# Megakernel of state space mixer and experts: one region of SBUF shared by all stages takes the first operands of the following stage, and the last stage's weights are split as a 33rd expert

## What is computed

```
x1  = x + tanh(g_x) * mamba(ctx, gate = layernorm(x))       # selective scan, 1024 channels x 16 states
xn  = layernorm(x1)
ffn = 2 * sum over 4 chosen of 32 experts (w1, w3: 1024x512; w2: 512x1024; at most 256 rows in each)
      + shared expert (w_sg, w_su: 1024x1024; w_sd: 1024x1024)
out = x1 + tanh(g_f) * ffn
```

## Time and profile before

| what | value |
|---|---|
| median of three runs | 4308.99 us |
| profiled execution, its own time | 4307.87 us |
| its span in the profile | 4306.1 us |
| TensorE busy | 3887.4 us (90%) |
| VectorE busy | 3074.7 us (71%) |
| ScalarE busy | 2147.3 us (50%) |
| GpSimd busy | 1800.7 us (42%) |
| barrier passed into the scan | 567.15 us |
| into the first shared pass | 1842.42 us |
| into the experts (first issue of SP) | 2539.66 us |
| into the second shared pass | 3725.18 us |

### The profile page before, as it was taken

How to read it: one execution, slowest core, us unless ns; L and a number is a source line. 1 busy time by engine, 2 the same in 40 slices (tenths; PEclk the granted TensorE clock), 3 DMA queues, 4 the chain that set the end, 5 groups by cost and what they waited for, 6 DMA issues and landing times. The chain is left out here.

```text
span 4306.1 us, 59367 instructions
## 1 busy us (share of the span) xinstructions
PE 3887.4 (90%) x21088; PEld 3143.6 (73%) x21088; DVE 3074.7 (71%) x3700; ACT 2147.3 (50%) x2213; POOL 1800.7 (42%) x1010
## 2 busy tenths in 40 slices
PE   8877548888988889869999979999999999899999
...
GB/s 230 215 232 225 181 219 118 106 200 118 108 209 107 138 181 114 89 189 187 188 171 182 192 179 243 234 229 230 232 230 231 229 232 232 174 293 249 200 161 122
DMA packets 327334, 817.74 MB, mean 190 GB/s; under 512 B 66112, under 2 KB 108352, under 8 KB 317952
## 3 DMA queue, kind: packets, MB, share of 16 engines
...
...
## 5 line engine op out<-in xcount | busy, mean ns | idle before, releaser
L926 POOL TENSOR_TENSOR h<-h,c 128x1024 f32<-128x1024 f32 x512 | 1206.4, 2412 | 54.8 <-DVE h L909 52.1
L909 DVE TENSOR_TENSOR_SCAN h<-da,dbu 128x1024 f32<-128x1024 f32 x512 | 1134.7, 2273 | 74.1 <-ACT dbu L875 51.4
L943 PE MATMUL psb<-m,du_taps 128*128 128x128 f32 x4096 | 581.5, 290 | 130.2 <-ACT dbu L875 80.4
L943 PEld LDWEIGHTS psb<-m,du_taps 128*128 128x128 f32 x4096 | 511.0, 196 | 197.5 <-ACT dbu L875 109.2
L882 ACT ACTIVATE da<-dl,ad 128x1024 f32<-128x1024 f32 x512 | 589.6, 1151 | 79.5 <-DVE h L909 67.4
L953 PE MATMUL psy<-ident,h 128*128 128x128 f32 x4096 | 562.1, 281 | 46.5 <-POOL h L926 27.0
L875 ACT ACTIVATE dbu<-psb 128x1024 f32<-128x1024 f32 x512 | 523.1, 1022 | 83.6 <-PE psb L943 72.1
L1822 DVE TENSOR_TENSOR wsp<-raw,wsp 128x2048 fp32r<-128x2048 f32 x192 | 434.1, 2289 | 106.7 <-ACT wsp L1775 106.7
L953 PEld LDWEIGHTS psy<-ident,h 128*128 128x128 f32 x4096 | 447.6, 143 | 81.4 <-POOL h L926 54.2
L1662 POOL DMA_INDIRECT xg<-scratch_xn,ids x64 | 63.6, 993 | 1054.8 <-PE psT L1682 1033.0
L1775 ACT ACTIVATE wsp<-raw 128x2048 fp32r<-128x2048 f32 x192 | 359.1, 1910 | 17.4 <-DMA raw<-in_w 16.9
...
## 6 DMA issues: line engine op xcount, KB each, us to landing
raw<-in_w SPq DMA_DIRECT2D x192, 1024.0 KB, 6.9
du_taps<-scratch_duT SPq DMA_DIRECT2D x512, 128.0 KB, 2.9
scratch_duT<-duT SPq DMA_DIRECT2D x64, 512.0 KB, 2.7
c<-scratch_c SPq DMA_DIRECT2D x64, 512.0 KB, 8.7
...
scratch_ob<-ob SPq DMA_DIRECT2D x64, 512.0 KB
...
xz<-in_x SPq DMA_DIRECT2D x32, 512.0 KB, 5.6
```

The source lines that it names most:

```text
L909: dve.tensor_tensor_scan(h[:, k % HR, :], da[k % 2][:, :], dbu[:, (k // GN) % 2, k % GN, :], 0.0, ALU.mult, ALU.add).then_inc(s_scan, 1)
L926: pool.tensor_tensor(h[:, k % HR, :], h[:, k % HR, :], c[:, n, :], ALU.mult).then_inc(s_hc, 1)
L943: mm = pe.matmul(psb[:, j], duT[:, r * CP + j, :], m[:, g // 2, :, r * CP + j, g % 2 * GN:(g % 2 + 1) * GN], start=True, stop=True)
```

## The change

- A region `arena` of 48 KB in each partition is allocated once and kept. In stage 1 it holds `w_in` and `ctxT`; in stage 2 the first half of the matrix (`m0`, 32 KB) and the taps (16 KB) lie in its place; in stage 3 `raw` and the token tiles `xt` and `xin`; in stage 4 `raw` and the transposed rows; in stage 5 `y` and the transposed tokens. `ident` is loaded once, in stage 1.
- Stage 1, in drain steps, all from SP: at step 33 `zero_matrix` (zeros to `m0`, 4 MB, from the 1 KB of `zero`), at steps 36 and 37 `first_du` (1 MB each, two DMAs), at step 40 `first_matrix` (8 DMAs of 128 KB). In the scan the second half `m1` is zeroed by GpSimd and loaded behind c[0] to c[2].
- Stage 2, last unit, before its last store: `first_weights` (4 MB) and `first_tokens` (four tiles, 2 MB).
- Stage 3, before the stores of tile 30: `first_expert`, w1 and w3 of expert 0 (4 MB).
- Stage 4: the second half of the shared expert is loaded and split as expert 32, its third matrix at an additional place in the last expert; the first transposed tokens are loaded after the last up product. `wsp` is handed on to stage 5, which splits nothing, and its memset of `y` waits for nothing.
- The semaphores of the early loads are cleared once, at the end.

In the diff's middle parts `early`, once the name of a flag in `split`, becomes `second`; those lines and some of names and waits are cut.

```
+            def zero_matrix():
+
+                sp.wait_ge(s_psx, Q)
+                sp.wait_ge(s_zero, 1)
+                sp.dma_start(f32(m0[:]).rearrange("p (r z) -> p r z", z=ROW), zero[:].unsqueeze(1).to_broadcast([P, TB, ROW])).then_inc(s_mz, 16)
+
+            def first_matrix():
+
+                sp.wait_ge(s_mz, 16)
+                sp.wait_ge(s_btst, 4 * P // TB * 16)
+                for dst_, src_ in matrix_blocks(f32(m0[:]).rearrange("p (t r) -> p t r", t=TB), dr, 0, 0):
+                    sp.dma_start(dst_, src_).then_inc(early["m"], 16)
+
+            def first_du(part):
+
+                for q in s_dust:
+                    sp.wait_ge(q, 16)
+                for twin in range(2):
+                    sp.dma_start(f32(taps[part * 2 * TB + twin:(part + 1) * 2 * TB:2]), dr["duT"][0, twin]).then_inc(early["du"], 16)
+
             def step(s):
                 on_tile(s, LOG + 1, store_delta)
+                if s == Q + 1:
+                    zero_matrix()
+                if s == Q + 4:
+                    first_du(0)
+                if s == Q + 5:
+                    first_du(1)
+                if s == Q + 8:
+                    first_matrix()
...
+def matrix_blocks(m, dr, b, half):
+
+    for part in range(2):
+        for a in range(TB // BAND):
+            band = dr["bT"][b, part, half]
+            rows = bass.AP(band.tensor, band.offset + a * BAND * SKEW, [[BAND * ROW, 2 * BAND], [1, BAND * ROW]])
+            p0 = part * 2 * TB + a * 2 * BAND
+            yield m[p0:p0 + 2 * BAND, a * BAND:(a + 1) * BAND].rearrange("p t r -> p (t r)"), rows
...
-        m = sb("m", [P, 2, TB, NC, NH], F32R)
-        duT = sb("du_taps", [P, NC, P], F32R)
+        m0, m1 = m0[:], sb("m", [P, TB * ROW], F32R)[:]
+        m = [v.rearrange("p (t c n) -> p t c n", t=TB, c=NC) for v in (m0, m1)]
...
+            def first_weights():
+
+                sp.wait_ge(s_mm, (NU - 1) * NST + NH)
+                for mat, src_ in enumerate((io["w_sg"], io["w_su"])):
+                    for half in range(2):
+                        w0 = (2 * mat + half) * KH * HB // 2
+                        sp.dma_start(arena[:, w0:w0 + KH * HB // 2].rearrange("p (k f) -> p k f", k=KH // 2),
+                                     src_[:, 0:HB].rearrange("(h k p) f -> h p k f", h=2, p=P)[half]).then_inc(early["w3"][mat][half], 16)
+
+            def first_tokens():
+
+                sp.wait_ge(s_mm, SETS)
+                sp.wait_ge(s_gst, 16 * ET)
+                for t in range(2):
+                    for i, src_ in enumerate((dr["gated"], io["x"])):
+                        w0 = 2 * KH * HB + (2 * i + t) * H
+                        sp.dma_start(arena[:, w0:w0 + H], src_.rearrange("b (t p) h -> (b t) p h", p=P)[t]).then_inc(early["x"][t], 16)
+
             load_delta(0)
-            for r in range(PARTS):
-                load_du(0, r)
-            load_m(0, 0)
-            load_c(0, 0)
+            for n in range(3):
+                load_c(0, n)
             load_m(0, 1)
-            for n in range(1, NST):
+            for n in range(3, NST):
                 load_c(0, n)
...
+                if final:
+                    first_weights()
+                    first_tokens()
...
             act.dma_start(gate[:], io["g_x"].partition_broadcast(P)).then_inc(s_c, 16)
-            act.dma_start(ident[:], io["ident"]).then_inc(s_c, 16)
-            act.wait_ge(s_c, 32)
+            act.wait_ge(s_c, 16)
             act.activation(gate[:], gate[:], ACT.Tanh).then_inc(s_gate, 1)
...
-            dve.memset(f32(m[:, 0]), 0.0).then_inc(s_zero, 1)
...
-            pool.memset(f32(m[:, 1]), 0.0).then_inc(s_zero, 1)
+            pool.memset(f32(m1), 0.0).then_inc(s_zero, 1)
...
-            pe.wait_ge(s_c, 32)
...
                 if g == 0:
-                    pe.wait_ge(s_du[r], i * 64 + 64)
-                if k % (ET * NST) in (0, NH):
-                    pe.wait_ge(s_m[k % (ET * NST) // NH], (i // ET + 1) * 2 * TB // BAND * 16)
+                    if i:
+                        pe.wait_ge(s_du[r], i * 64)
+                    elif r == 0:
+                        pe.wait_ge(early["du"], 64)
+                half = k % (ET * NST) // NH
+                if k == 0:
+                    pe.wait_ge(early["m"], 2 * TB // BAND * 16)
+                elif k % (ET * NST) in (0, NH):
+                    pe.wait_ge(s_m[half], (i // ET + half) * 2 * TB // BAND * 16)
...
-            consts = [(gate[:], io["g_f"].partition_broadcast(P)), (ident[:], io["ident"])]
+            consts = [(gate[:], io["g_f"].partition_broadcast(P))]
...
-            load(0, 0)
+            cols = slice(0, HB)
             if route:
-                load(1, 1)
-            cols = slice(part * HB, (part + 1) * HB)
-            for m, src in enumerate((io["w_sg"][:, cols], io["w_su"][:, cols], io["w_sd"][cols, :])):
...
                 for half in range(2):
-                    if m == 2:
-
-                        sp.wait_ge(s_wlo, half + 1)
-                    sp.dma_start(raw[:, m % 2, halves[half]].rearrange("p (k f) -> p k f", k=blocks),
-                                 src.rearrange("(h k p) f -> h p k f", h=2, p=P)[half]).then_inc(s_raw[m % 2][half], 16)
+
+                    sp.wait_ge(s_wlo, half + 1)
+                    sp.dma_start(raw[:, 0, halves[half]].rearrange("p (k f) -> p k f", k=KF // 2),
+                                 io["w_sd"][cols, :].rearrange("(h k p) f -> h p k f", h=2, p=P)[half]).then_inc(s_raw[half], 16)
             if route:
                 sp.wait_ge(s_init, 1)
                 sp.dma_start(dr["tab"].rearrange("(p s) o -> p (s o)", p=P), zero[:]).then_inc(s_tab, 16)
...
+            def first_expert():
+
+                sp.wait_ge(s_wlo, 6)
+                for m, src in enumerate((io["w1"], io["w3"])):
+                    for half in range(2):
+                        sp.dma_start(raw[:, m, halves[half]].rearrange("p (k f) -> p k f", k=KH // 2),
+                                     src[0].rearrange("(h k p) f -> h p k f", h=2, p=P)[half]).then_inc(early["w4"][m][half], 16)
+
...
+                    if route and known and t == TT - 2:
+                        first_expert()
...
-                    pool.wait_ge(s_x[par], j * 32 + 32)
+                    if isinstance(j, int) and j == 0:
+                        pool.wait_ge(early["x"][par], 32)
+                    else:
+                        pool.wait_ge(s_x[par], j * 32)
...
-                pool.wait_ge(s_wlo, 6)
...
-                    if first:
+                        if known and t == 0:
+                            pe.wait_ge(early["xT"], 16)
+                        else:
+                            pe.wait_ge(s_x[par], j * 16 + 16 * par)
+                    if route and first:
...
             if route:
                 x_head(0, 0, 0)
-            for m in range(3):
-                for half in range(2):
...
+            if route:
+                for m in range(3):
...
-                src = (io["w1"], io["w3"], io["w2"])[m][e].rearrange("(h k p) f -> h p k f", h=2, p=P)
+                if isinstance(e, int) and e == NE:
+                    src = (io["w_sg"][:, HB:FS], io["w_su"][:, HB:FS], io["w_sd"][HB:FS, :])[m]
+                else:
+                    src = (io["w1"], io["w3"], io["w2"])[m][e]
+                src = src.rearrange("(h k p) f -> h p k f", h=2, p=P)
...
-            load_matrix(0, 0, 0)
-            sp.dma_start(ident[:], io["ident"]).then_inc(s_c, 16)
...
-            load_matrix(0, 0, 1)
             load_matrix(0, 0, 2)
             load_matrix(1, 1, 0)
...
-                    load_matrix(e + 1, x + 1, 1)
-                    load_matrix(e + 1, x + 1, 2)
-                if not (known and e + 2 >= NE):
+                load_matrix(e + 1, x + 1, 1)
+                load_matrix(e + 1, x + 1, 2)
+                if not (known and e + 2 > NE):
                     load_matrix(e + 2, x + 2, 0)
+                if known and e == NE - 1:
+
+                    sp.wait_ge(s_u, TPE * NE)
+                    sp.dma_start(xT[:, 0].bitcast(F32), dr["xT"][0]).then_inc(early["xT"], 16)
                 store_rows(e, 0)
...
-                    act.wait_ge(s_raw[c][half], ((3 * e + m) // 2) * 16 + 16)
+                    if isinstance(e, int) and e == 0 and m < 2:
+                        act.wait_ge(early["w4"][m][half], 16)
+                    else:
+                        act.wait_ge(s_raw[c][half], ((3 * e + m) // 2) * 16)
...
-                if not last:
-                    matrix_head(e + 1, x + 1, 0)
+                matrix_head(e + 1, x + 1, 0)
                 silu(e, 1)
-                if not last:
-                    matrix_head(e + 1, x + 1, 1)
+                matrix_head(e + 1, x + 1, 1)
...
+                if last:
+                    matrix_head(e + 1, x + 1, 2)
...
-                if not last:
-                    for half in range(2):
-                        matrix_rest(e + 1, x + 1, 0, half)
```

(36 more changed lines are left out.)

99 lines of the change are left out of this document (45 added, 54 removed).

## The result

Over four runs each, the kernel after took 4251.88 us (4248.17 to 4255.61) and the kernel before 4308.65 us (4304.97 to 4309.22): the ratio is 0.987, with a 95% interval of 0.9853 to 0.9887. In the profiled executions the span falls from 4306.1 to 4253.8 us, by 52.3.

What follows compares the result with a forecast made beforehand. TensorE, busy 90% of the span, paces shared passes and experts, VectorE and GpSimd the scan; only stage boundaries could gain. Terms -19.3 +1.0 +0.5 +2.8 -2.4 -5.0 -13.6 +2.7 +0.5 gave -32.8: 4276 us, range 4269 to 4291.

Steps and rivals of the forecast that it cites:

- Scan, the gain: Barrier into the scan to first scan: first matrix and taps already in place, first scan at +15.0 for +34.3, -19.3 us.
- Scan, the price: End of stage 1: new SP transfers delay the stores behind them; zeros +1.0, taps +0.5, matrix +2.8 us.
- rival (a): End of stage 1: zeros crawl at 131 GB/s, price 21 us in place of 1, time 4296; chance 0.08.
- First shared pass: Head of stage 3: loads removed, norm earlier, but last gated store lands later behind the preloads; -2.4 us (-6 to +1).
- experts: Head of stage 4: first transpose waits for the gather, no longer for the identity; -5.0 us (-3 to -6).
- second pass: Head of stage 5: first product needs only gate and transposed tokens, 3727.5 in place of 3741.12; -13.6 us.
- the last expert: End of stage 4: third split of the 33rd expert delays the copy of psO; +2.7 us (0 to 5).
- (c): Rival: preloads given back where issued, every upper price at the other steps, 9 us dearer, time 4285; chance 0.22.
- (b): Rival, end of stage 1: zeros so slow that the kernel gets slower, at 60 GB/s about 4335 us; chance 0.03.
- (d): Rival, scan's head: c rows or u hold the ladder, 2 to 6 us more, 4281; 0.65 together with the forecast.
- (e): Rival, stage boundaries: no change, because stages hide their heads; chance 0.02.
- the third sign: Sign of being wrong: TensorE stays longer at the lower clock in the new heads than in the old; same loss assumed.

## Why the prediction was wrong

**The step that failed** is the sentence in the first part that "inside the stages nothing of the change could help much", because TensorE sets the pace there. That it sets the pace was right, and is the reason why the change helped: with TensorE busy 350.00 of 350.00 us, anything that makes one product cheaper goes straight to the end. I took the duration of a product as a property of its shape, 128x128 with 512 columns, and counted what was added, removed and moved in time, but not what was moved in space. The change lays every tile of stages 3 to 5 anew. One pair, `xT_place` and wsp, came to stand at the same place within 256 bytes, and its 4,608 products went from 233 to 227 ns: 26 of the 52.3 us. Moving one against the other by 32 bytes undoes it, moving both keeps it, and giving the other pairs the same distance gains some 16 us more. No row of the kernel before could price it, as all its pairs stood 32 bytes off; that the layout was changed under the engine that bounds three stages could have been named as a case, and wasn't.

**Scan, the gain** (-19.3, measured -18.6): right. The 0.7 is the gate's load: I took 4.1 us to the tanh, it was 5.2.

**Scan, the price** (+4.3, measured +10.0, and 10.6 with the preloads taken out): the mechanism was right and the sizes too small, in all three: zeros +1.0 (measured 3.9), taps +0.5 (2.7), matrix +2.8 (4.3). Zeros: I took 392 GB/s from the clearing of the bands. Windows of the kernel after while the zeros move:

```profile
480.00:484.00 4.00, 0.00 (x0) 0.00 (x0) 2.20 (x2) 3.98 (x4) 2.34 (x1) 0.50 1.00 284
...
546.00:552.00 6.00, 1.97 (x8) 1.57 (x8) 4.28 (x4) 3.22 (x4) 1.48 (x2) 0.50 1.04 131
```

In the two windows that follow the first there are 286 and 287 GB/s. At some 285, SBUF to SBUF with the DMA engines fully busy, 4.19 MB take 14.7 us and not 10.7. The transfer landed 17.6 us after its issue, so the first of the signs of being wrong, zeros over 15 us, was seen, and du_head(21), which was to wait 1 us or less, came 3.9 late. The rival (a), 131 GB/s, did not happen. Matrix: the last of these rows is its load, at exactly the 131 GB/s that I took. The Trainium skill, page "SBUF — State Buffer", section on the DMA port swizzle, measures 104 GB/s for 1 MiB over partitions 0 to 15; the trace has 131, over a matrix whose eight DMAs of 128 KB each write another 16 partitions, which is not quite the same case. So its rate was right, and still the stores behind it were later than forecast: issued at 547.64, they landed in 7.8 us. Taps and matrix together cost 5.6 us by the run without the transfer of zeros, 7.0 by the delta sums, where 3.3 were forecast. For the taps the DMA issues of the first of their two steps (from 511 to 518; count, KB each, us to landing) say why:

```profile
du_taps<-scratch_duT SPq DMA_DIRECT2D x2, 512.0 KB, 6.8
scratch_duT<-duT SPq DMA_DIRECT2D x2, 512.0 KB, 8.0
```

I gave the transfer 5.3 us and 2 to 3 us of slack; it took 6.8, in the second step 8.0, and the stores behind it land in 8.0 and 7.8 us, where such a store takes 2.7. No window has the taps' transfer alone, so its own rate stays unmeasured.

**First shared pass** (-2.4, measured -1.9), **experts** (-5.0, -5.3), **second pass** (-13.6, -13.3) **and the last expert** (+2.7, +2.1): right, each by the mechanism named. The last gated store did stand behind the weights: 9.27 us to the next stage's first issue for 4.59, a price of 4.7 where I said 3.0. In the other executions with these preloads it is 3.1 to 4.0, so the 3.0 was near; but its sum was loose, since 1823.3 + 16.0 + 1.3 gives 1840.6 and not 1842.3.

**The rivals.** Of (c), upper prices everywhere, the part in stage 1 came nearly true (its upper prices were taps 3 and matrix 5; measured 2.7 and 4.3), with zeros that cost 3.9 on top; the rest did not. (b), (d) and (e) did not happen: the scan took 1229.4 us from its first step to its last, for 1230.0. Nor did the third sign, apart from 1 us: at the heads of the experts and of the second pass 13 and 12 products follow one another at 0.43 us in place of 0.23, for 8 and 11 in the kernel before. Without the faster products the result would have been near 4278 by the windows. The kernel with `xT_place` moved is a run of just that: its ratio puts it at 4288 (4281 to 4295), at the high end of the range, 4291. So the forecast of "faster" was safe on the boundaries alone, but their gain was 20 to 31 us and not 32.8; that 4252 lies below the range is due to the layout, and this part of the gain was luck.
